# A causal mask written into PSUM by ScalarE instead of added by TensorE, in four of twelve score groups

## What is computed

```python
q, k, v = split_heads(sn_dense(layernorm(x), W_qkv))       # 16 heads of width 8
att = einsum('bhqd,bhkd->bhqk', q, k) * scale              # [32, 16, 256, 256]
att = where(causal == 0, finfo.min, att)                   # causal mask
att = softmax(att, axis=-1)
x = x + sn_dense(einsum('bhqk,bhkd->bhqd', att, v), W_proj)
```

## Time and profile before

| | |
|---|---|
| median of 3 runs | 1045.26 us (1042.62 to 1045.6) |
| profiled execution | 1035.15 us, span of its instructions 1033.3 us |
| mean granted TensorE clock | 0.955 |
| busy share: PE, DVE, POOL, ACT | 87%, 70%, 66%, 59% |

### The profile page before, as it was taken

The page is one execution under the profiler, slowest core; times in us unless marked ns, Lnnn a source line. Parts: engine busy times, 40 slices in busy tenths (PEclk is TensorE's granted clock), DMA queues, the critical chain, the costliest instruction groups (busy, mean ns, idle before and its releaser), DMA issues. The chain is left out here.

```text
span 1033.3 us, 26499 instructions
## 1 busy us (share of the span) xinstructions
PE 896.4 (87%) x8219; PEld 679.6 (66%) x8219; DVE 724.8 (70%) x2368; ACT 607.5 (59%) x1581; POOL 682.8 (66%) x1247
## 2 busy tenths in 40 slices
PE   5937499999647999999999999999999873999995
PEld 5823399999623566565656666565656542999995
DVE  8879745444237889899998989998898845444441
ACT  2637366666313666676666666666666651766662
POOL 7709668643023678888888888888887773355554
PEclk9999799999958999999999999999999985999998
DMA  7450022223145544446354554545454102222220
GB/s 214 128 173 1 17 69 67 69 66 64 40 79 106 122 96 101 115 94 122 95 116 101 109 108 97 121 95 117 95 115 97 39 24 61 60 67 67 64 59 21
DMA packets 127407, 89.72 MB, mean 87 GB/s; under 512 B 14305, under 2 KB 117910, under 8 KB 127270
## 3 DMA queue, kind: packets, MB, share of 16 engines
q1 hardware_dynamic: 103078, 52.69, 22.8%
q10 hardware_dynamic: 15488, 17.74, 7.7%
q0 software_dynamic: 8704, 17.60, 6.6%
HBM read 52.23 MB, written 35.47 MB: 85 GB/s over the span
## 5 line engine op out<-in xcount | busy, mean ns | idle before, releaser
L1291 ACT ACTIVATE at_pt<-at_pm 128x512 f32<-128x512 f32 x384 | 228.5, 598 | 117.9 <-PE at_pm L1379 84.2
L1609 DVE TENSOR_REDUCE at_mx<-at_pp 128x2 f32<-128x512 f32 (+1 forms) x384 | 259.5, 678 | 44.7 <-PE at_pp L1368 37.1
L1207 POOL TENSOR_SCALAR_AFFINE_SELECT at_pt<-at_pt 128x256 f32<-128x256 f32 (+1 forms) x384 | 187.8, 493 | 57.4 <-ACT at_pt L1291 54.1
L925 ACT ACTIVATE e_ht<-e_ps_h,b1t 128x128 f32<-128x128 f32 x576 | 164.8, 370 | 98.2 <-PE e_ps_h L954 98.2
L964 PE MATMUL e_ps_y<-w,e_ht 128*128 x1152 | 159.2, 282 | 0.0
L954 PE MATMUL e_ps_h<-e_xnt,e_w1own 128*128 128x128 f32 x1152 | 154.8, 279 | 1.4 <-issue 1.4
L954 PEld LDWEIGHTS e_ps_h<-e_xnt,e_w1own 128*128 128x128 f32 x1152 | 143.0, 195 | 1.6 <-issue 1.6
L964 PEld LDWEIGHTS e_ps_y<-w,e_ht 128*128 128x128 f32 x1152 | 140.0, 192 | 1.7
L1011 DVE SCALAR_TENSOR_TENSOR e_y<-e_ps_y,e_x 128x256 f32<-128x256 f32 x72 | 30.6, 425 | 155.7 <-PE e_ps_y L964 155.7
L888 POOL DMA_INDIRECT out_dram<-e_y,e_x x72 | 73.6, 1022 | 86.4 <-DVE e_y L1011 74.8
L1400 PE MATMUL at_po<-at_pt,vp 128*32 128x256 f32 (+1 forms) x2048 | 109.8, 332 | 1.6 <-POOL at_pt L1207 1.6
(11 more groups left out here) (327 smaller groups left out, 1788.6 us busy)
## 6 DMA issues: line engine op xcount, KB each, us to landing
at_qkd<-at_part SPq DMA_DIRECT2D x64, 192.0 KB, 3.0
kb<-at_qkd SPq DMA_DIRECT2D x64, 96.0 KB
qs<-at_qkd ACTq DMA_DIRECT2D x64, 96.0 KB
e_x<-buckets SPq DMA_DIRECT2D x72, 66.0 KB, 1.9
x<-e_y SPq DMA_DIRECT2D x36, 128.0 KB, 1.8
rows<-ts_x ACTq DMA_DIRECT2D x16, 264.0 KB, 3.0
ts_x<-in_x_dram SPq DMA_DIRECT2D x16, 256.0 KB, 3.5
x_by_token<-at_xa SPq DMA_DIRECT2D x32, 128.0 KB
```

Of the source, the lines that this page charges most:

```text
L925: last = a.activation(hid_t[j % NB][:, f, :], ps_h[j % NB][:, f, :], ACT.Gelu, bias=c.b1t[:, ds(e, 1), f])
L1207: g.affine_select(out=tile, in_=tile, compare_op=ALU.is_ge, fill=0.0, base=0, pattern=[[0, n], [1, P]], channel_multiplier=-1).then_inc(ma ...
L1291: a.activation(pt[u % RING][:, :], pm[u % 2], ACT.Exp, scale=SCALE).then_inc(exped, 1)
L1609: v.tensor_reduce(out, src, axis=AX.X, op=ALU.max).then_inc(maxed, 1)
```

## The change

In the first four groups (v = 0 to 3) of every sequence but the first, PE no longer multiplies the mask into the bank. ACT copies `c.mask` into `pp[v % 2]` first, right after the exponential of step u = v + 4, once the maximum of group v - 2 is taken, and raises `filled`. PE waits for `filled` instead of `maxed`, and its two matmuls add their scores to what stands in the bank (`start=False`). In the steps u = 5 to 8, where these groups lie, PE does scores by key before scores by query.

```diff
+        kept, filled = [sem(f"kept{k}") for k in range(2)], sem("filled")
@@ scalar engine, in turn(), right after the exponential of step u
+                    if u in (4, 5, 6, 7) and has(2) and b + 2 > 0:
+                        n, w = b + 2, u - 4
+                        wait(act, maxed, n * NP + (w - 1))
+                        a.activation(pp[w % 2], c.mask[:, :, :].rearrange("p a q -> p (a q)"), ACT.Copy).then_inc(filled, 1)
@@ tensor engine, scores_by_query
+                    if v < 4 and n > 0:
+                        wait(pe, filled, 4 * (n - 1) + (v + 1))
+                        for w in range(2):
+                            last = te.matmul(out[:, w * S:(w + 1) * S], qs[s][0:ROWS, 2 * v + w, 0:P], kb[s][0:ROWS, 2 * v + w, :, 0:P],
+                                             start=False, stop=(w == 1), skip_group_check=True)
+                        last.then_inc(pre_done, 1)
+                        return
                     wait(pe, maxed, n * NP + (v - 1))
@@ tensor engine, the steps of a turn
                 for u in range(NP):
+                    if has(0) and 5 <= u <= 8:
+                        scores_by_key(u)
                     for o, v in QUERY_TILES[u]:
                         if has(o):
                             scores_by_query(o, v)
-                    if has(0):
+                    if has(0) and not 5 <= u <= 8:
                         scores_by_key(u)
```

More of the change, by code:

```diff
@@ L1094, in attention @@
              "num_out").split())
-        kept = [sem(f"kept{k}") for k in range(2)]
+        kept, filled = [sem(f"kept{k}") for k in range(2)], sem("filled")
         size, wnorm_d, tiny, far = two("size", [P, TPB]), sb("wnorm_d", [P, E]), sb("tiny", [P, TPB, E]), sb("far", [P, TPB, E], BF16)
```

## The result

The change makes the kernel slower: 1066.47 us (median of 4 runs, 1066.03 to 1066.94) against 1044.46 us (4 runs of the kernel before), a ratio of 1.0212, 95% interval 1.0198 to 1.0227. That is +22.0 us; +22.5 and a time of 1067.8 were predicted. The profiled execution took 1066.55 us.

What follows compares the result with a forecast made beforehand. The bound was a chain of PE (9.5 us) then DVE (6.8 us) per turn; ACT's copies delay PE by 0.82. Three partial turns (1.2) and 26 full ones (21.3) add 22.5 us: 1067.8, range 1045 to 1083.

Steps and rivals of the forecast that it cites:

- PE's piece: Part of a turn from L1415 until group 5 reaches DVE's maximum: 9.5 us before, 0.82 us longer with the change.
- DVE's piece: Part of a turn from group 5's maximum to the next L1415: 6.8 us, not shortened by waiting.
- What bounds: A turn of attention is one closed chain: PE for 9.5 us, then DVE for 6.8 us, plus hand-overs.
- the late L1475: PE's L1475 in u = 8 waits for ACT's L1324 until 597.83 and comes 0.81 us late.
- The masks taken away: Four mask matmuls off PE, 0.22 us each, 0.88 us a turn; with the copies added this buys nothing.
- The copy: Four 128x512 copies on ACT, SBUF to PSUM: 0.60 us long, step 0.49, bounds 0.44 to 0.57; 1.96 us a turn.
- the walk: Step-by-step timing of PE and ACT through u = 4 to 8: group 5 0.82 us later, turn 17.3 us; 70 in 100.
- The sum: Whole kernel: 1.2 us for turns 1, 2 and 29, 21.3 for 26 full turns at 0.82; together +22.5 us.
- The base: The median of runs lies 10 us above the profiled execution; the same 22.5 us is added to it, giving 1067.8.
- No gain: Against the rival that copies hide in ACT's idle third: 1026 us at a step of 0.1, chance 13 in 100.
- The formula behind that rival: Delay a turn is 0.82 - 4 x (0.49 - step): a gain at copy steps under 0.285 us.
- the third rival: Slower by more: PE idles in u = 5, 6 and 8, its clock falls; 1093 us, chance 5 in 100.

Runs made afterwards that it cites:

- The spare copies: Kernel before plus four ACT copies of the mask to unread SBUF tiles after the exponentials of u = 4 to 7, masks kept on PE: 1067.35 us, ratio 1.0207.
- the two spare-copy kernels: Kernel before plus four unread mask copies on ACT, at u = 4 to 7 (1067.35 us) or at u = 1, 3, 9 and 10 (1045.62 us).
- 32 columns: Changed kernel with only the first 32 columns of each bank filled by ACT's copies, the other columns' mask left out: 1038.82 us, ratio 0.9952.
- the order alone: Kernel before with scores by key ahead of scores by query in steps 5 to 8, masks still multiplied on PE: 1039.51 us, ratio 0.9954.
- 256 columns: Changed kernel with only the first 256 columns of each bank filled by ACT's copies, the other columns' mask left out: 1050.64 us, ratio 1.0067.
- the kernel of before with narrow maskings: Kernel before with POOL's 128x512 masking of every third step cut to one of four blocks: 1043.45 us, ratio 0.9977.
- early fills: Kernel before with ACT filling only groups 0 and 1, earlier, around the exponential of u = 4: 1039.2 us in new PE order, 1040.75 in old.
- the narrow masking: POOL's 128x512 masking cut to one of four blocks, on the kernel where ACT fills group 1 alone (1028.99 us) and on the kernel before (1043.45 us).

## Why the prediction was right, step by step

| step of the prediction | predicted | the profile after |
|---|---|---|
| length of a copy, its step | 0.60, 0.49 | 0.60, 0.52 (525.13 to 525.65) |
| group 0, after the transposes | 2.17 | 2.26 |
| group 1 | 4.15 | 4.18 |
| `times_v` | 4.46 | 4.50 |
| group 3 | 6.85 | 6.87 |
| L1475 (L1486) | 7.25 | 7.24 |
| group 4 | 8.10 | 8.10 |
| PE's piece | +0.82 | +0.83 |
| DVE's piece | unchanged | -0.20 |
| the turn | 17.3 | 17.16 |

- **What bounds.** Right: one chain of PE's piece and DVE's piece, and within PE's the late L1475. The spare copies show it directly, since they lengthen PE's piece by 0.84 without touching PE.
- **The masks taken away.** Right that they buy nothing here. What they are worth with nothing in their place was put too high, at 0.88: the kernel without them shows 0.64 on PE's piece.
- **The copy.** The form that no row of before had, SBUF to PSUM, steps by 0.52 like SBUF to SBUF, not by 0.49 like PSUM to SBUF. Four copies add 0.12 to the walk by that. It came out right because L1324 (L1320 before) steps by 0.07, not by 0.13, and several other steps are 0.01 to 0.02 shorter than in it. That is luck of 0.12 us a turn, or 3 us in the sum. The estimate from the page "Perfetto Trace Analysis" of the Trainium skill (a step of 0.45 if writing PSUM counted like reading it) is not borne out; the measurement decides. The difference that the page gives by what is read is there: 0.52 from SBUF, 0.48 to 0.50 from PSUM.
- **DVE's piece.** This step failed: "its own piece of 6.8 us isn't shortened by waiting". It was 6.97 before as a median (the turn shown had 6.81) and 6.76 after. DVE's idle time before the maxima, 15.3 us in 150 above, or 1.75 a turn, was 1.11 a turn before:

```profile
L1609 DVE TENSOR_REDUCE at_mx<-at_pp 128x2 f32<-128x512 f32 (+1 forms) x110 | 74.4, 676 | 10.1 <-PE at_pp L1368 10.0
```

  That is the growth of the turn, 0.64, and not the 0.8 that PE's piece alone would give. What the 0.20 come from can be read too. DVE runs without a gap in both, but L1568 (L1581), with two inputs in SBUF, meets a masking of POOL in most turns of before (16 of 21) and in few of after. DVE and POOL in a turn of before, then DVE of after:

```profile
537.62 0.57 DVE L1568 SCALAR_TENSOR_TENSOR at_weight<-at_aff,at_amax,down 128x8 f32<-128x8 f32 x2
```
```profile
537.76 0.41 POOL L1207 TENSOR_SCALAR_AFFINE_SELECT at_pt<-at_pt 128x256 f32<-128x256 f32 x1 [0.77 <-ACT at_pt L1291]
```
```profile
537.38 0.36 DVE L1581 SCALAR_TENSOR_TENSOR at_weight<-at_aff,at_amax,down 128x8 f32<-128x8 f32 x2
```

  The median of the second of its two instructions fell from 0.42 to 0.21 us, and that of the first one of the normalisation behind it from 0.56 to 0.40; against that L1572 (L1585) grew from 0.19 to 0.38. So the part that the prediction held constant moved with the meetings of DVE and POOL, which it left out of account.
- **The sum.** The size of this term was off, and the ends made up for it. From b = 4 to 27, 24 turns took 412.5 us instead of 397.2: 0.64 each, 15.3, where 24 x 0.82 is 19.7. The two turns ahead of them, b = 2 and 3, taken at 0.4 and 0.82, grew by 1.10 and 1.28 (15.38 to 16.48, 16.25 to 17.53), and those behind by 1.4 together. From the first L1415 to the last that makes 19.1, and 0.4 more lie between the start of attention and the first L1415. The other 2.5 of the 22.0 lie in the measurement (the interval reaches from 20.7 to 23.7) or behind the loop, and are not placed: behind the last L1415 the profile of the changed kernel takes 181.5 us and that of before 177.9, but the other kernels, with the same code there, take 179.0 to 181.9. So the +22.5 is better than its terms.
- **The base.** Right to add the difference to the median and not to the profiled execution: the two profiled spans differ by 31.5 us. The profiled execution of before was ahead by some 8 us where attention starts (284.1 us, against 291 to 293 in all the others), and the change doesn't touch that stretch. Profiles of the two spare-copy kernels, with spans of 1065.0 and 1043.0, differ by 22.0.
- **The rivals.** No gain: a copy of 512 columns steps by 0.52. The formula behind that rival, -4 us of delay a turn for each us of step, holds only near its start: 32 columns step by 0.12 (532.17 to 532.29 on ACT), for which it gives 0.66 less than before, and PE's piece fell by 0.22 at best; the whole kernel was no faster than with the order alone. Even from the full copy to 256 columns (a step of 0.31) PE's piece falls by 3 us for each us of step, not by 4. The clock stayed at 1.00 from 500 to 650 us with PE busy 135.66 of 150, so the third rival fell too. Over the whole program it was 0.924 in this profile and 0.955 in that of before, but that isn't the loss: an execution of the changed kernel at 0.951 took 1066.03 us, those at 0.924 and 0.925 took 1066.38 to 1066.94.

What stays open: why L1301 comes 0.25 to 0.57 us late in some turns. It is seen with the order alone and with the copies in several lengths; in the changed kernel it mostly ends before the exponential of u = 4 is due, as in the turn shown (0.74 after L1426, the exponential still at 1.02), and it lengthens 2 of 19 turns by 0.3. In the kernel before it is never late. Open too is what delays the load of `qs` in the kernel of before with narrow maskings.

## What to carry to other kernels

An engine with a third of its time idle can still be full for the six microseconds in which another engine waits for it: four copies of 0.5 us cost 22 us in one set of steps and nothing in another. So before moving work, find who waits last in the half of the loop in question, walk the steps of the receiving engine one by one to that wait, and use the step from start to start, not the duration. A spare copy for which nobody waits, put at the planned places, measures the cost of such a move ahead of the change itself. And check after each run who is last now: the narrow masking made DVE 0.3 to 0.4 us faster in two kernels, and only in one of them was DVE still the one that PE waited for.

## What the runs showed of the hardware that was not expected

- A masking of POOL, 128x512, holds a DVE instruction with two inputs in SBUF until it ends: 0.61 us for four elements a partition instead of 0.16, 0.98 for a normalisation instead of 0.67. DVE's maxima, which read PSUM, stay within 0.67 to 0.69 in DVE's piece. This agrees with the page "SBUF — State Buffer" of the Trainium skill, section "SBUF: two separate sides": a DVE instruction with two SBUF inputs and a GpSimd one that reads SBUF take the shared pair of ports as an exclusive lock for the whole instruction. What it means for a loop is that DVE's piece moves with the phase of two engines: 6.76 us in the changed kernel and 7.11 with early fills, 2% of a turn, for the same work on DVE and on POOL.
- ACT from bf16 in SBUF takes 0.60 to 0.61 us for 128x512 into PSUM and 0.63 into SBUF (628 ns mean), but holds the engine 0.52 either way (525.13 to 525.65 and 530.21 to 530.73). Duration and step go apart.
